# The interpolation of a slot's chunk moved from the middle of VectorE's slot to its end

## The reference, cut to what matters

```python
x = x + grouped_conv3x3(_gn(x), W, b)            # 8 groups; its output is reordered between pixels and channels
g = _gn(x)                                       # group norm, 32 groups
h = relu(bn1(conv1x1(g)))                        # 512 -> 128 channels
off = conv3x3(h)                                 # 18 channels: dy and dx of 9 taps
# for each of 9 taps and each pixel: four neighbours of h at (y + ky + dy, x + kx + dx)
val = v00*wy0*wx0 + v01*wy0*wx1 + v10*wy1*wx0 + v11*wy1*wx1
d = einsum('bckhw,ock->bohw', val, w_def) + b    # deformable convolution
x = x + relu(bn3(conv1x1(bn2(d))))               # 128 -> 512 channels
```

## Time and profile before

| what | us |
|---|---|
| median of 3 runs (lowest, highest) | 1888.68 (1883.96, 1896.87) |
| the profiled execution | 1897.85 |
| its span, first to last instruction | 1896.0 |
| coordinates of one image to those of the next (L646 at 899.97 and 1010.74) | 110.77 |

### The profile page before, as it was taken

How to read it: one execution, slowest core, us unless ns; L and a number is a source line. 1 busy time by engine, 2 the same in 40 slices (tenths; PEclk the granted TensorE clock), 3 DMA queues, 4 the chain that set the end, 5 groups by cost and what they waited for, 6 DMA issues and landing times.

```text
span 1896.0 us, 32497 instructions
## 1 busy us (share of the span) xinstructions
PE 1669.0 (88%) x10144; PEld 932.4 (49%) x10144; DVE 1415.9 (75%) x3450; ACT 965.2 (51%) x1475; POOL 1218.7 (64%) x1159
## 2 busy tenths in 40 slices
PE   2999998989989899998989999898989989897655
PEld 1555454655545464554546455454645545463321
DVE  4448787787868788786878878787787868777664
ACT  5665544555555555565455555544555654432212
POOL 0007776767767676766767676676667767677774
PEclk9999998999999999998999999998999999898776
DMA  6026776777677687877768687776768777676875
GB/s 214 1 108 188 224 218 215 254 222 252 205 240 227 219 253 223 259 222 238 216 215 254 216 266 225 241 209 220 241 218 258 214 244 218 184 240 205 268 217 162
DMA packets 142458, 412.99 MB, mean 218 GB/s; under 512 B 24518, under 2 KB 25030, under 8 KB 142150
## 3 DMA queue, kind: packets, MB, share of 16 engines
q0 software_dynamic: 92160, 302.06, 53.7%
q1 hardware_dynamic: 49814, 106.27, 14.9%
q10 hardware_dynamic: 304, 2.44, 0.6%
HBM read 339.37 MB, written 71.30 MB: 217 GB/s over the span
## 4 chain that ended last, share of the span: by engine, by line
PE 40%; DMA 17%; DVE 14%; issue 14%; POOL 10%; ACT 5%; POOLq 0%; ACTq 0%; DVEq 0%
PE bank L741 18%; DMA sb_rows<-table,sb_ridx 16%; POOL sb_rows L322 10%; PE bank L723 7%; PE bank L755 4%; DVE sb_val L547 4%; DVE sb_rows L539 3%; PE bank L714 3%; ACT sb_split L398 2%; PE bank L773 2%; PE bank L730 2%; DVE sb_split L580 2%; PE bank L830 2%; ACT sb_norm L391 1%; PE bank L808 1%
## 5 line engine op out<-in xcount | busy, mean ns | idle before, releaser
L322 POOL DMA_INDIRECT sb_rows<-table,sb_ridx x1152 | 1216.7, 1056 | 636.3 <-issue 423.4
L539 DVE SCALAR_TENSOR_TENSOR sb_rows<-sb_rows,sb_frac 128x256 f32<-128x256 f32 x1152 | 509.4, 480 | 281.3 <-DMA sb_rows<-table,sb_ridx 276.3
L741 PE MATMUL bank<-sb_split,sb_wg 128*128 128x512 f16 x2304 | 574.5, 397 | 67.3 <-ACT sb_h_sb L424 44.5
L741 PEld LDWEIGHTS bank<-sb_split,sb_wg 128*128 128x128 f16 x2304 | 223.7, 100 | 365.3 <-issue 142.0
L547 DVE SCALAR_TENSOR_TENSOR sb_val<-sb_rows,sb_frac 128x128 f32<-128x128 f32 x1152 | 329.3, 348 | 15.3
L723 PE MATMUL bank<-sb_valT,sb_wd 128*128 128x512 f32 x576 | 330.1, 657 | 0.0
L352 ACT ACTIVATE sb_valT<-bank 128x512 f32<-128x512 f32 x288 | 170.7, 593 | 295.4 <-PE bank L714 294.8
L370 ACT ACTIVATE sb_conv_sb<-bank,sb_bias 128x512 f32<-128x512 f32 x256 | 173.5, 684 | 217.2 <-PE bank L741 179.4
L714 PE MATMUL bank<-sb_eye_sb,sb_val 128*128 128x128 f32 x1152 | 186.1, 286 | 109.1 <-DVE sb_val L547 89.1
L755 PE MATMUL bank<-sb_fold_sb,sb_conv_sb 128*64 128x64 f32 x4096 | 261.5, 281 | 1.7 <-ACT sb_conv_sb L370 1.6
L755 PEld LDWEIGHTS bank<-sb_fold_sb,sb_conv_sb 128*64 128x64 f32 x4096 | 244.2, 207 | 31.1 <-issue 27.9
(11 more groups left out here) (76 smaller groups left out, 1019.9 us busy)
## 6 DMA issues: line engine op xcount, KB each, us to landing
table<-sb_table_sb SPq DMA_DIRECT2D x144, 256.0 KB, 4.6
sb_xs<-x SPq DMA_DIRECT2D x64, 512.0 KB, 9.5
out<-sb_res SPq DMA_DIRECT2D x128, 256.0 KB, 4.0
sb_rows<-table,sb_ridx POOLq DMA_INDIRECT x1152, 4.2
sb_rows<-w_group ACTq DMA_DIRECT2D x2, 1152.0 KB, 13.8
sb_wd<-w_def SPq DMA_DIRECT2D x1, 576.0 KB
sb_w<-w_in SPq DMA_DIRECT2D x1, 256.0 KB
sb_w<-w_out SPq DMA_DIRECT2D x1, 256.0 KB
```

Of the source, the lines that this page charges most:

```text
L322: pool.indirect_dma_start(out=rows[:, (c % RING) * PER + i, :], out_offset=None, in_=tables[u % 2], in_offset=bass.IndirectOffsetOnAxis(ap ...
L539: op = nc.vector.scalar_tensor_tensor(r[:, 0:2 * CH], r[:, 2 * CH:4 * CH], frac[:, parity, half * PER + i, k, 0:1], r[:, 0:2 * CH], ALU.mu ...
L741: op = nc.tensor.matmul(pair_ps[half][:, :], wg[:, g, k, :], plane(split1[:, g, :], ky + half * HROWS, kx, HROWS), start=k == 0, stop=k == ...
```

## The change: two calls change places

In every slot of DVE the call of `interpolate` goes from its place behind `add_shuffled` to the end of the slot, behind `differences`. Nothing is added or left out, and no other engine's program changes.

```diff
--- before.py
+++ after.py
@@ -679,10 +679,6 @@
                             add_shuffled(new, (u + 2) % XBUFS, *SHUFFLE[s - 1])
                         else:
                             add_shuffled(nxt, (u + 1) % XBUFS, *SHUFFLE[s - 1])
-                    image, back, c = chunk_at(s, 0, t, tail, b)
-                    if image is not None:
-                        interpolate(image, (u - back) % 2, c)
-
                     if a2 and s in STATS:
                         statistics2(STATS[s])
                     if a2 and s in VAR2:
@@ -699,6 +695,10 @@
                         coordinates()
                     if a2 and s == H_SLOT + 1:
                         differences()
+
+                    image, back, c = chunk_at(s, 0, t, tail, b)
+                    if image is not None:
+                        interpolate(image, (u - back) % 2, c)
 
             run(dve, step)
```

## The result

The changed kernel takes 1916.41 us (median of 4 runs, 1906.58 to 1928.11) beside 1890.99 for the kernel before: ratio 1.0138, 95% interval 1.0071 to 1.0206. The profiled execution took 1915.88 us, its span is 1914.1. I forecast 1882 us and no clear change; it came out as the slower rival had it (1903 to 1917), a little above my range.

What follows compares the result with a forecast made beforehand. PE, busy 88%, and POOL, nearly as full, bind through a loop of waits. Per image 0.7 + 2.7 + 1.0 - 4.05 = 0.35 us, 5 us in 14 images, plus 2: 1888.7 becomes 1882, range 1836 to 1913.

Steps and rivals of the forecast that it cites:

- the slower rival: Slot 17: differences ahead of chunk 10 make PE wait longer, clock drops behind both gaps; 1903 to 1917 us; chance 0.22.
- Items 1 to 4: Waits on PE: 8.4 us of gaps an image go; 1.1, 3.2, 3.4 us come back before chunks 6, 7, 10.
- item 2: low1 ahead of chunks 3, 5, 7, 9: new PE gaps, 1.1 us before chunk 6 and 3.2 before chunk 7.
- Item 5: POOL's gathers for chunks 11 and 12: the long gather stays held under differences; PE's waits of 2.2 us go.
- Item 6: statistics2, scale2, add_residual, coordinates ahead of chunks: run inside DVE's waits or delay chunks PE wants later; taken as nothing.
- the clock's term of the sum: PE's lower clock behind gaps: an image wins 2.7 + 1.0 us, loses 4.05 as three in four new gaps drop.
- The won drop: Lower clock behind PE's 3.49 us wait for h, at the convolution and product: 2.7 us an image won back.
- the three signs: Prediction wrong if gap before chunk 7 is under 2 us, before chunk 10 over 5, or PE's clock moves over 0.02.
- The faster rival: PE's new gaps do not lower the clock: 48 to 62 us gained, 1827 to 1841 us; chance 0.32.

Runs made afterwards that it cites:

- f2: The kernel before, with differences alone moved ahead of the interpolation: 1846.87 us, ratio 0.9773 to the kernel before.
- f3: The kernel before, with variance2 and bias_of_h alone moved ahead of the interpolation: 1837.34 us, ratio 0.9724 to the kernel before.
- g3: The changed kernel, with low1 alone put back behind the interpolation: 1854.75 us, ratio 0.9779 to the kernel before.
- g1: The kernel before, with statistics2, scale2, add_residual and coordinates alone moved ahead of the interpolation: 1891.28 us, ratio 0.9986 to the kernel before.
- f1: The kernel before, with low1 alone moved ahead of the interpolation: 1995.12 us, ratio 1.055 to the kernel before.
- f0: The changed kernel, unaltered, timed again beside the runs of its parts: 1920.22 us, ratio 1.0174 to the kernel before.
- g2: The changed kernel, with 12 unused matmuls in each of PE's gaps before chunks 7 and 10: 1858.55 us, ratio 0.9804 to the kernel before.

## Why the prediction was wrong

**Items 1 to 4, the waits, were right** to some tenths. The gaps of 1.07, 0.70 and 0.94 went; those before chunks 6, 7 and 10 came at 1.2, 3.2 and 3.0 us (1.1, 3.2 and 3.4 forecast); the wait for `h` went whole. Two small slips stand in the working: PE's lead at chunk 7 is by item 2's own numbers 951.51 - 950.8 = 0.7 us, not 1.0, and the gap before chunk 10 is 980.6 - 977.1 = 3.5, not 3.4. My 0.7 us less idle time an image, 9.8 us in 14, looks like the 10.1 of the whole span, but that agreement is partly luck: PE idles 14.2 us less between the first and the last L646, 1.0 an image, and 4.3 us more at the end. With the measured gaps my own sum gives 8.4 - 7.4 = 1.0.

**Item 5 was right in kind.** The long gather stayed, once an image, and ended 0.8 us behind the differences. The two waits for chunks 11 and 12 went. That a gather issued under the differences is always held to their end is not so: in f2, f3 and g3 most ended behind an earlier one of the four. The sum did not see that the gather could be had short, some 4 us of POOL's time an image.

**Item 6 was right**: g1 shows nothing for the small items, within 0.4%.

**The step that failed is the clock's term of the sum**: 2.7 + 1.0 won, 4.05 lost, 0.35 us an image, 5 us more busy time of PE in all. It was 28.2 us, 23.1 of them between the first and the last L646. Three numbers in it were wrong, all to one side. The won drop I took at 2.7 us from the one step of the rows. It was among the longest: by the table of lines the convolutions' busy time fell from 574.5 to 552.0 us, 1.6 an image, and with the product behind it is about 2.1 (the granted clock says the same: half of PE's busy time in these low stretches is 27.6 us, in 13 images). The drop at chunk 7 I let happen three times in four; it happened in all 14 images, and it cost 3.0 each, for it fell on the densest work of the step. Before, then after:

```profile
L808 PE MATMUL bank<-sb_xs,sb_w_norm 128*128 128x512 f32 x256 | 116.6, 598 | 1.1 <-ACT sb_w_norm L414 1.1
L818 PE MATMUL bank<-sb_gs,sb_w 128*128 128x1 f32 x128 | 15.2, 240 | 0.0
...
L808 PE MATMUL bank<-sb_xs,sb_w_norm 128*128 128x512 f32 x256 | 151.3, 747 | 1.1 <-ACT sb_w_norm L414 1.1
...
L818 PE MATMUL bank<-sb_gs,sb_w 128*128 128x1 f32 x128 | 22.8, 299 | 0.0
```

That is 34.7 + 7.6 = 42.3 us in 14 images. The drop at chunk 10 came in 10 of 14, at 2.9 us by the granted clock. With these, 14 x 3.0 + 10 x 2.9 = 71 us lost against 14 x (2.1 + 1.0) = 43 won: 28 us where I had 5. That this meets the 28.2 so closely is partly chance: all these gaps lie between the first and the last L646, where PE's busy time grew by 23.1 us, and drops in other places changed too and stand in neither sum.

**The signs.** None of the three signs by which I called the prediction wrong came true: the gap before chunk 7 was not under 2 us, the one before chunk 10 not over 5, and PE's mean clock moved by 0.016 (0.948 to 0.932), not by 0.02. The last was too coarse to be a sign: 0.02 of the span is 38 us.

**The rivals.** The slower one had the time (1903 to 1917) and its condition, a drop behind both gaps. It named the differences at chunk 10 as the mechanism; f2 shows that they gain by themselves. They cost only where something else brings PE earlier to chunk 10, and the gap that costs more is chunk 7's, behind `low1`: f1, and g3 against f0 (with the long gather as a second difference there). The faster rival needed gaps without a drop: g2 makes exactly that, and gives 1858.6 us where I had 1827 to 1841. The overpriced old drop is 8 us of the difference; what the rest is, the filling matmuls themselves among it, is not shown.

I had the rows to do better. From the first L646 to the last, every gap of PE of 2.4 us or more in the trace before was followed by half clock; the earlier trace rows show one each, 3.49 and 3.08 us. I argued the new ones down to three in four because dense matmuls stood around them. Taking each gap as followed by a drop would have given the slower rival as the forecast. It would have been right in sign and too sure: 4 of the 28 gaps had none.

## What to carry to other kernels

When engines wait for each other in a ring, price a reordering by PE's gaps one by one, and behind each gap of the size that was followed by half clock before, add the lost work of what then runs; this second term decided here. Take that price from the mean over all images, not from the one step that is read closely. Move only the items that some engine waits for (`variance2`, `bias_of_h`) and leave behind the chunk those that themselves wait (`low1` for ACT): moving everything turned a gain of 2.8% into a loss of 1.4 to 1.7% on the chips at 1890 us. Each order has to be read on POOL too: the long gather stayed in the whole change and vanished in f2, whose expectation had it only come free earlier.

## What the runs showed of the hardware

- The lower clock behind a gap costs about as much as the gap: 3.0 us of lost work behind gaps of 2.6 to 3.3 us at chunk 7. It followed in 24 of 28 cases (26 of 28 in the profile of f0), also between dense products, and unused matmuls in the gaps gave back 61.7 us.
- One program took 1890 us on one chip and 2124 to 2139 us on three others, and the ratio of the changed kernel to the one before went from 1.017 to 0.996 with it. The verdict of a schedule as tight as this one holds for the chip that it was timed on.
- A gather that POOL issues while DVE subtracts one SBUF tensor from another can take 5.70 us, not 0.95, and then ends 0.8 us behind the last of four such operations (15 cases in the kernel before, 14 in the changed one). It need not: in f3 (11 images) and g3 (13) it took 1.6 to 1.7 us and ended 0.8 us behind the first of the four. From g3, with the first of the four from 740.62 to 742.01:

```profile
741.10 1.72 POOL L322 DMA_INDIRECT sb_rows<-table,sb_ridx  x1 [0.30 <-issue]
743.23 0.94 POOL L322 DMA_INDIRECT sb_rows<-table,sb_ridx  x1 [0.41 <-issue]
```

  What decides between the two stays open.
